# Routing in two mixture layers: normalisation per token, top two from raw logits, and another order of the steps around it

## The reference, cut to what matters

```python
x = x + 0.5 * _L0_ffn_ref(_layernorm(x, axis=-1), ...)    # F
x = x + _L0_attn_ref(_layernorm(x, axis=-1), ...)         # S
x = x + 0.5 * _L0_ffn_ref(_layernorm(x, axis=-1), ...)    # F
x = x + 0.5 * _L1_ffn_ref(_layernorm(x, axis=-1), ...)    # M
x = x + _L1_attn_ref(_layernorm(x, axis=-1), ...)         # U
x = x + 0.5 * _L1_ffn_ref(_layernorm(x, axis=-1), ...)    # M

def _L1_ffn_ref(x, w_router, w1, b1, w2, b2):             # 8 experts, top 2
    logits = xf @ w_router
    probs = jax.nn.softmax(logits, axis=-1)
    topk_w, topk_idx = jax.lax.top_k(probs, TOP_K)
    ...
    out = jnp.sum(out * weights[..., None], axis=1)
```

## Time and profile before

| | us |
|---|---|
| median of three runs | 1194.48 |
| lowest and highest run | 1188.43, 1200.24 |
| the profiled execution | 1189.11 |
| its span | 1187.3 |

### The profile page before, as it was taken

The page is one execution under the profiler, slowest core; times in us unless marked ns, Lnnn a source line. Parts: engine busy times, 40 slices in busy tenths (PEclk is TensorE's granted clock), DMA queues, the critical chain, the costliest instruction groups (busy, mean ns, idle before and its releaser), DMA issues.

```text
span 1187.3 us, 25908 instructions
## 1 busy us (share of the span) xinstructions
PE 1012.3 (85%) x9070; PEld 632.4 (53%) x9070; DVE 720.2 (61%) x1625; ACT 688.2 (58%) x1301; POOL 524.8 (44%) x405
## 2 busy tenths in 40 slices
PE   4788999999998876799999999999639968746995
PEld 1345555555555364355555555555339964325995
DVE  0577678777776653677776776876564423654441
ACT  2566686686673662676677667656316636623661
POOL 2664456556441542545444344433345530263451
PEclk9899999999999967999999999999759989857997
DMA  9895344455433600545444344432312240011223
GB/s 349 250 298 157 86 102 109 97 120 116 100 93 81 71 1 2 126 109 121 96 107 96 89 107 109 101 80 77 143 44 68 67 114 1 19 43 48 64 65 120
DMA packets 88511, 120.02 MB, mean 101 GB/s; under 512 B 20064, under 2 KB 72032, under 8 KB 87488
## 3 DMA queue, kind: packets, MB, share of 16 engines
q1 hardware_dynamic: 81824, 96.30, 33.8%
q0 software_dynamic: 6272, 20.44, 4.7%
q10 hardware_dynamic: 288, 1.63, 0.3%
HBM read 62.66 MB, written 22.11 MB: 71 GB/s over the span
## 4 chain that ended last, share of the span: by engine, by line
PE 65%; ACT 14%; issue 7%; DMA 6%; DVE 5%; POOL 1%; SPq 1%; ACTq 0%; DVEq 0%; POOLq 0%
PE banks L591 7%; PE banks L944 6%; PE banks L954 6%; PE banks L676 5%; PE banks L662 5%; PE banks L620 3%; PE banks L751 3%; PE banks L669 3%; PE banks L637 3%; PE banks L721 3%; PE banks L726 2%; PE banks L645 2%; DMA rstd<-arena 2%; ACT arena L1194 2%; ACT arena L1189 2%
## 5 line engine op out<-in xcount | busy, mean ns | idle before, releaser
L2041 POOL TENSOR_TENSOR arena<-arena 128x1024 f32<-128x1024 f32 x64 | 150.9, 2357 | 321.0 <-DVE arena L1644 318.7
L2030 POOL TENSOR_TENSOR arena<-arena 128x1024 f32<-128x1024 f32 x64 | 150.8, 2357 | 41.6 <-ACT arena L1189 41.6
L1636 DVE TENSOR_REDUCE arena<-banks 128x4 f32<-128x512 f32 x128 | 82.5, 686 | 93.5 <-PE banks L620 93.3
L1181 ACT ACTIVATE arena<-banks,arena 128x512 f32<-128x512 f32 x128 | 80.5, 679 | 93.6 <-PE banks L669 93.2
L591 PE MATMUL banks<-arena 128*128 128x512 f32 x256 | 128.6, 627 | 6.7 <-DVE arena L1563 5.9
L2020 POOL DMA_INDIRECT moe_outs<-arena x78 | 81.5, 1045 | 100.7 <-DVE arena L1882 88.6
L1386 ACT ACTIVATE arena<-banks,arena 128x128 f32<-128x128 f32 x312 | 89.0, 369 | 59.0 <-PE banks L944 58.9
L2013 POOL DMA_INDIRECT moe_rows<-arena x64 | 63.1, 986 | 118.5 <-DVE arena L1617 101.1
L1644 DVE TENSOR_TENSOR arena<-arena 128x1024 f32<-128x1024 f32 x64 | 78.1, 1220 | 28.4 <-DMA arena<-arena 28.4
L1194 ACT ACTIVATE arena<-banks 128x1024 f32<-128x1024 f32 x64 | 65.6, 1025 | 46.1 <-PE banks L591 45.1
L954 PE MATMUL banks<-arena 128*128 x624 | 87.5, 283 | 4.6 <-ACT arena L1386 4.4
(11 more groups left out here) (221 smaller groups left out, 1951.6 us busy)
## 6 DMA issues: line engine op xcount, KB each, us to landing
arena<-arena SPq DMA_DIRECT2D x256, 128.0 KB, 3.8
arena<-rstd SPq DMA_DIRECT2D x128, 256.0 KB, 4.3
moe_rows<-arena POOLq DMA_DIRECT2D x12, 903.0 KB, 6.6
arena<-moe_rows SPq DMA_DIRECT2D x78, 64.5 KB
arena<-in_rot SPq DMA_DIRECT2D x4, 1024.0 KB, 11.6
arena<-in_mw SPq DMA_DIRECT2D x2, 2048.0 KB, 10.8
arena<-moe_outs SPq DMA_DIRECT2D x16, 256.0 KB, 4.9
arena<-ssm_a SPq DMA_DIRECT2D x4, 512.0 KB, 6.6
```

The costliest lines, as they stand in the source:

```text
L1636: nc.vector.tensor_reduce(mx[:, e], by_row(bank[3 + e][:]), AX.X, ALU.max).then_inc(s_max, 1)
L2030: nc.gpsimd.tensor_tensor(TA[:, n % 2], RAW, ROTV[:, :, 0, c * C:(c + 1) * C], ALU.mult).then_inc(cos_done, 1)
L2041: nc.gpsimd.tensor_tensor(TA[:, n % 2], TA[:, n % 2], TB, ALU.add).then_inc(rot_sum, 1)
```

## The change

- The router weights are centred once: WRC = centre x WR, a matmul on PE (`centred_router`, L565 of the changed kernel) and a copy by DVE (L1546). The router's matmuls take X as it is and WRC (L571).
- The four transposes become four matmuls of X's tiles with `centre` (`token_rows`, L577), so tokens stand on partitions, centred but not yet scaled. DVE takes mean and variance of each token by `bn_stats` and `bn_aggr` (`moments`, L1572, L1576). ACT makes the inverse root of 128x4 values for a chunk and scales in the copy to XTOK: four copies of 128x128 for the first choice; the second choice is one copy of 128x512 from the first.
- The top two are taken from the unscaled logits (`pick`, L1553 to L1565: 5 chained steps in place of 10). The softmax of all tokens comes once for a mixture, `gates_start` behind the tile map, an exponential on ACT, and `gates_end` ahead of the diagonals.
- POOL scatters a chunk's four first choices when the first copy and the ranks are there, then the four second ones.
- The steps stand in another order on PE, DVE and ACT, in the tail of the second F as well as in U. Banks: `MX_TOK` and `MX_RANK` take the place of `MX_CEN` and `MX_VAR`.

```diff
@@ PE
+            def centred_router():
+                pe.wait_ge(moe_s_in, 48)
+                mm(bank[1][:, 0:NE], centre, WR, start=True, stop=True).then_inc(wrc, 1)
+
+            def route(moe, c):
+                pe.wait_ge(wrc, 2)
                 for t in range(TILES):
                     at = c * C + t * P
-                    last = mm(bank[MX_VAR[moe][c]][:, t * NE:(t + 1) * NE], YB[:, at:at + P], WR, start=True, stop=True)
+                    last = mm(bank[MX_RANK[moe][c]][:, t * NE:(t + 1) * NE], X[:, at:at + P], WRC, start=True, stop=True)
                 last.then_inc(router_mm, 1)
+
+            def token_rows(moe, c):
                 for t in range(TILES):
                     at = c * C + t * P
-                    last = nc.tensor.transpose(bank[MX_CEN[moe][c]][:, t * P:(t + 1) * P], YB[:, at:at + P], ident)
+                    last = mm(bank[MX_TOK[moe][c]][:, t * P:(t + 1) * P], X[:, at:at + P], centre, start=True, stop=True)
                 last.then_inc(xtok_mm, 1)
...
                     elif run:
                         pe.wait_ge(copied, 2 * n)
+                        pe.wait_ge(sq_done, n)
+                        centred_router()
                         pe.wait_ge(x_ffn, NCH + 1)
-                        centred(X, 0, MX_CEN[0][0])
+                        token_rows(0, 0)
...
                 if run:
-                    variance(mix, 0, MX_VAR[0][0])
+                    route(0, 0)
                 transpose_out(29, n - 3, s)
                 masks(31, n - 1)
                 values(30, n - 2, 0)
                 scores(31, n - 1)
                 values(30, n - 2, 1)
                 if run:
-                    pe.wait_ge(moe_s_in, 48)
-                    route(mix, 0, 0)
+                    rank(0, 0)
                 transpose_scores(31, n - 1)
...
                 unit_centred(3)
-                mix_centred(0)
-                mix_variance(0)
                 down(1)
+                enter(0)
                 unit_variance(3)
-                route(mix, 1, 0)
                 up(2, range(3))
-                mix_centred(1)
                 rank(1, 0)
-                mix_variance(1)
+                enter(1)
                 up(2, range(3, 4))
                 up(3)
-                route(mix, 1, 1)
+                rank(1, 1)
                 down(2)
                 down(3)
-                rank(1, 1)
-                mix_centred(2)
-                mix_variance(2)
-                route(mix, 1, 2)
-                mix_centred(3)
+                enter(2)
+                enter(3)
                 rank(1, 2)
-                mix_variance(3)
-                route(mix, 1, 3)
                 rank(1, 3)
@@ ACT
             def tokens(moe, c):
...
+                act.wait_ge(tok_dve, 2 * k + 2)
+                A(RSTD[:, tt], MOMENT[:, tt, 1], ACT.Ln, bias=eps_c).then_inc(tok_act, 1)
+                act.wait_ge(tok_act, 2 * k + 1)
+                A(RSTD[:, tt], RSTD[:, tt], ACT.Exp, scale=-0.5, bias=zero_c).then_inc(tok_act, 1)
...
+                for t in range(TILES):
+                    at = c * TILES + t
+                    last = A(XTOK[:, 0, at, 0:DM], bank[MX_TOK[moe][c]][:, t * P:(t + 1) * P], ACT.Copy, scale=RSTD[:, at:at + 1])
+                last.then_inc(xtok_done, 1)
+                act.wait_ge(xtok_done, 2 * k + 1)
+                A(XTOK[:, 1, tt, 0:DM], XTOK[:, 0, tt, 0:DM], ACT.Copy).then_inc(xtok_done, 1)
@@ DVE
                 normalise(31, n - 1)
                 if run:
-                    norm_chunks(mix, first_plain, [0])
+                    dve.wait_ge(cos_done, n)
+                    centred_router()
+                    moments(0, 0)
                 maximum(n - 1)
                 subtract(n - 1)
+                if run:
+                    pick(0, 0)
                 divide(n - 2)
-                if run:
-                    dve.wait_ge(cos_done, n)
-                    route(0, 0)
                 divide(n - 1)
...
                 if moe == 0:
-                    rank(0, 1)
-                    norm_chunks(norm0, first_plain, [2])
-                    route(0, 2)
                     rank(0, 2)
-                    norm_chunks(norm0, first_plain, [3])
-                    route(0, 3)
+                    pick(0, 3)
+                    moments(0, 3)
                     rank(0, 3)
                 tile_map()
+                gates_start(moe)
@@ POOL
-                    pool.wait_ge(xtok_done, 2 * k + 2)
                     pool.wait_ge(rank_dve, RANK_STEPS * (k + 1))
-                    for t in range(c * TILES, (c + 1) * TILES):
-                        for j in range(2):
+                    for j in range(2):
+                        pool.wait_ge(xtok_done, 2 * k + 1 + j)
+                        for t in range(c * TILES, (c + 1) * TILES):
```

More of the change, by code:

```diff
@@ L817, in ffn @@
                     pe.wait_ge(x_ffn, NCH + 2)
-                    centred(X, 1, MX_CEN[0][1])
+                    token_rows(0, 1)
+                    route(0, 1)
                 else:
@@ L830, in ffn @@
                 last_variance()
-                if run:
-                    variance(mix, 1, MX_VAR[0][1])
-                else:
+                if not run:
                     ssm_variance(0, 0)
@@ L837, in ffn @@
                 last_hidden(1)
-                if run:
-                    route(mix, 0, 1)
-                else:
+                if not run:
                     ssm_variance(1, 0)
                 last_hidden(2)
-                if not run:
+                if run:
+                    pe.wait_ge(xtok_done, 3)
+                    pe.wait_ge(rank_dve, 2 * RANK_STEPS)
+                    pe.wait_ge(x_ffn, NCH + 3)
+                    token_rows(0, 2)
+                    route(0, 2)
+                else:
                     ssm_centred(0, 1)
@@ L1289, in ffn @@
                 evacuate_out(31, n - 1, 0)
-                if run:
-                    norm_square(mix, 1, MX_CEN[0][1])
-                else:
+                if not run:
                     ssm_square(0, 0)
@@ L1310, in ffn @@
                 if run:
-                    tokens(0, 1)
+                    tokens(0, 2)
                 else:
@@ L1598, in route @@
[L1598 to L1600 removed]
+                for t in range(TILES):
+                    last = nc.vector.max(TOPL[:, c * TILES + t], part(moe, c, 0)[:, t])
+                chained(last, pick_dve)
+                for t in range(TILES):
+                    at = c * TILES + t
+                    last = nc.vector.max_index(TOPI[:, at], TOPL[:, at], part(moe, c, 0)[:, t])
@@ new lines, in pick, with moments @@
+                chained(last, pick_dve)
+                chained(nc.vector.tensor_copy(IDXF[:, tt], TOPI[:, tt]), pick_dve)
+                each = expert_id.unsqueeze(1).unsqueeze(1).to_broadcast([P, TILES, 2, NE])
+                chained(TT(OH[:, tt], each, IDXF[:, tt, 0:2].unsqueeze(3).to_broadcast([P, TILES, 2, NE]), ALU.is_equal), pick_dve)
+                chained(TT(MINE[:, tt], OH[:, tt, 0], OH[:, tt, 1], ALU.add), pick_dve)
+                assert n[0] == PICK_STEPS * (k + 1)
+            def moments(moe, c):
+                k = NCH * moe + c
+                dve.wait_ge(xtok_mm, k + 1)
+                for t in range(TILES):
+                    last = nc.vector.bn_stats(PART[:, c * TILES + t], bank[MX_TOK[moe][c]][:, t * P:(t + 1) * P])
+                last.then_inc(tok_dve, 1)
+                dve.wait_ge(tok_dve, 2 * k + 1)
+                for t in range(TILES):
+                    last = nc.vector.bn_aggr(MOMENT[:, c * TILES + t], PART[:, c * TILES + t])
+                last.then_inc(tok_dve, 1)
@@ L1763, in ffn @@
                 residual(7, gg - 1)
+                if run:
+                    pick(0, 1)
                 gate(6, gg - 2, 1)
+                if run:
+                    moments(0, 1)
                 gate(6, gg - 2, 2)
                 mlp_norm(7, gg - 1)
+                if run:
+                    rank(0, 1)
                 mlp_residual(6, gg - 2)
-                if run:
-                    norm_chunks(mix, first_plain, [1])
-                else:
+                if not run:
                     ssm_normed(0, 0)
@@ L1775, in ffn @@
                 if run:
-                    route(0, 1)
+                    pick(0, 2)
+                    moments(0, 2)
                 else:
```

174 lines of the change are left out of this document (66 added, 108 removed).

## The result

| | us |
|---|---|
| changed kernel, median of 4 runs (lowest, highest) | 1216.13 (1209.78, 1217.78) |
| kernel before, 4 runs beside them | 1191.86 (1188.43, 1200.24) |
| ratio, 95% interval | 1.0183 [1.0114, 1.0252] |
| the profiled execution after, its span | 1217.78, 1215.9 |

The changed kernel is slower by some 22 us (0.0183 x 1191.9; 14 to 30 by the interval), where the sum said 10.3. The two have most of their loss in common; that part is what the prediction is about. Whether the ratio itself differs is not shown, as the two intervals overlap; the traces of the two do differ.

The account below looks back on a forecast made before the run. PE's gapless chain in the second F's tail, then POOL's scatters, were taken as bounds. Terms: 22.6 - 10.7 - 1.6 = +10.3, giving 1199.4 from the profiled execution, 1204.8 by the median; 1202 put down, range 1189 to 1214.

Parts of the forecast that it names:

- C: Tail of second F: picks and ranks ahead of the last transposed scores, half clock included; +4.5, between 2.5 and 4.9.
- D: Rest of the tail: DVE's added picks, moments and ranks before the last residual, mostly fitting its waits; +2.1, 0 to 4.
- A: Head of step 32: PE waits for the router weights' load, then runs at half clock; +11.4, at least 9.0.
- B: Tail: copy of centred weights, router and three groups ahead of the last scores, half clock included; +4.6, 2.6 to 5.0.
- E: First routing's end: 16 back-to-back scatters, last starting 21.1 after the last residual in place of 31.8; -10.7.
- F: U and second routing: the scatter gap between chunks 2 and 3 goes, little else; -1.6, between -4 and +1.
- rival 2: Tail: clock doesn't recover between the three holes; +18.8, 1208 against the profiled execution, 1213 against the median; chance 0.18.
- Rival 3: Tail: PE's clock never falls at the waits; 6.4 less, so +3.9, 1193 and 1198; chance 0.15.
- Rival 4: Step 32: weights' wait is hidden by slack or they land at once; without A, -1.1; chance 0.12.
- slower by more than 12: Whole kernel: loss beyond the some 12 us that can be told from no change; chance 0.35.
- low end: Whole kernel: the terms' low ends sum to -0.6, giving 1188 from the lowest time; the range given starts at 1189.
- high end: Whole kernel: the terms' high ends, with -9.7 for the scatters, sum to +16.6, giving 1211 with the median.

Follow-up runs that it names:

- third group: Four old kernels run again unaltered on one chip: changed kernel 1202.40 (1.0126), kernel before 1185.62, and two partly moved-back versions, 1180.08 and 1189.42.
- third variant: Changed kernel with weights' wait, chunk 0's router, and chunk 0's picks and ranks moved back: 1192.79, 1.0016; timed again 1180.08, 0.9953.
- second group: Kernel before with three unused semaphores (1.0000); third variant with old semaphore order (0.9887), 8 unused columns (0.9950), or old scatter order (0.9936).
- first group: Four kernels undoing the changed kernel's moves one after the other, each keeping the earlier undoings: 1.0084, 1.0018, 1.0016, 1.0019 to the kernel before.
- first experiment: Changed kernel with the wait for the router weights moved from the head of step 32 to behind the loop: 1200.31, 1.0084.
- second variant: Changed kernel with the weights' wait behind the loop and chunk 0's router matmuls behind the last scores: 1193.02, 1.0018; timed again 1189.42, 1.0013.
- first variant: The kernel of the first experiment: changed kernel with only the weights' wait moved behind the loop, 1200.31, 1.0084.

## Why the prediction was right or wrong, point by point

Right: slower, for the reason given, three new waits of PE against back-to-back scatters. The size was short: 10.3 by the sum, 22 and 15 measured. Every term of the tail was too small, C and D most, and one cost was not in the profile of before at all. "First" is the trace of the result against the first of the kernel before, "again" the same pair in the third group (the three waits by their marks in the chains, the rest by the stretches).

| term | predicted | first | again |
|---|---|---|---|
| A, weights' wait | +11.4 | +12.2 | +12.0 |
| B, router ahead of the scores | +4.6 | +5.3 | +5.2 |
| C, ranks ahead of the transposed scores | +4.5 | +5.8 | +5.8 |
| D, rest of the tail | +2.1 | +5.3 | +3.3 |
| E, scatters behind the residual | -10.7 | -10.2 | -10.4 |
| F, U and second routing (U and R) | -1.6 | +9.8 | -0.9 |
| sum | +10.3 | +28.2 | +15.0 |

The sums leave out X (+3.5 and -3.1) and the moment at which the tail is reached (3.0 earlier, 1.7 later). With these the spans differ by 28.6 and 13.7.

- **A** was worked out as the wait and 2.4 for the clock, and came out nearly so (810.20 less 798.12, against 800.96 less 801.13: 12.2). The clock's part was 2.8 and not 2.4. The last load landed in 4.54 and 4.30. The Trainium skill ("DMA: Bandwidth & Descriptors", section "Anatomy of one DMA — SWDGE (gpsimd) path") has 2.0 as the fixed part alone and adds bytes / 436e9; for these 512 KB that would be 3.2, an estimate by that page, and 1.0 less than the trace's 4.2, not 2.2 as the prediction has it. The section is also about DMAs issued by GpSimd, and this one is SP's. Either figure is too short here.
- **B and C** ran at half clock nearly from end to end. Their clock cost 2.8 and 2.4 where 2.0 was put down; in C two records of L731 behind the transposed scores still took 1.71, not 0.86. C has a misreading as well: the transposed scores of before could go on behind the first half of the difference, not at 811.60, its end. Their row on PE's time line before:

```profile
811.06 1.25 PE L669 MATMUL banks<-arena 128*128 128x128 f32 x8
```

The picks now stand behind both halves, so 0.5 more is lost.
- **D** was too small (2.1; 3.3 again, and 5.3 first, where 1.89 is a late semaphore). The moments had the price forecast (0.89 + 0.38, predicted 1.4), but "most of the new work fits where DVE waited for PE" does not hold for the picks: in the third variant of the third group chunk 1's stand in the chain between output and gate (821.87 to 823.67). Without the three waits and without late semaphores T is still 2.3 (second group, three traces) to 3.7 (third group) above the kernel before. Moving chunk 1's work back won 1.2 in the first group, where semaphores were late in both traces; what the rest of D consists of is not isolated.
- **E** held to 0.5, with 21.6 predicted as 21.1. The chunks' second copies never held POOL up.
- **F** is the step that failed in the first trace. Without late semaphores it is -0.9 in the one pair: the last sum came 2.0 earlier, the last scatter 1.1 later behind it. That is partly luck. The last scatter was forecast 33 behind the sum and came 34.6 behind it in all six traces of the new routing without late semaphores (33.4 to 33.5 before), so this part costs 1.2 and wins nothing; and U is 156.3 to 163.9 in these six, so its -2.0 says little. With late semaphores the 8.6 of one update turned the sign. No row of before shows such a wait.
- **The rivals.** The clock doesn't stay low from B on (it is 1.00 at 824), so rival 2 falls, although the time came near its 1208 and 1213; the same number would have been taken for it without the stretches. Rival 3 falls with the stretches at 0.50: PE's pieces behind the three waits take 6.3, 6.4 and 6.0 (803.88 to 810.20, 817.25 to 823.61, 827.94 to 833.95), where the same ones at full clock take 3.6 and 3.5 by the prediction's rows and 3.6 in the third variant, so 8.0 together. The Trainium skill ("TensorE: Matmul & The Clock Gate", section "What's actually happening") advises leaving such ramps out, as under 1% of a span. The trace agrees with the share (0.7%), and yet it is over half of the 15 that the change costs. Rival 4 falls with the first experiment.
- **The number.** 1187.1 + 15.0 = 1202.1 is what these terms would give in the third group, and it measured 1202.4; that they meet so well is luck, as X and the arrival at the tail are left out. The recorded median, 1216.13, lies above the range's 1214, and the loss of 22 is the case "slower by more than 12", which had 0.35. By the prediction's own sum the low end is 1188 and not 1189, and the -9.7 of its high end has no working.
- **The difference between the two timings**, 14 us in the time and 7 us in the ratio, goes with late semaphores in the traces: 2.0 in D and 10.7 in F. The two waits without a releaser in the first trace (1.89 and 8.78) make 10.7 of these 12.7, and U's 2.0 are a part that I can't assign. Three kernels were timed both with late semaphores and without. The third variant's ratio fell clearly (1.0016 to 0.9953), the changed kernel's by as much but with overlapping intervals, and the second variant's not at all (1.0018 and 1.0013). So that the late semaphores make up the difference in time is argued and not shown, and what makes them late is open.

## What to carry to other kernels

Ask of every step that is moved forward what it waits for, and pay in full for the links behind it on an engine that has no gap there; add the clock that falls meanwhile (2.4 to 2.8 us here), once for each hole. A part of a change can be worth more than the change: the scatters' gain of 10 was real, and three small moves back kept it and made a kernel faster than both. When a ratio doesn't follow a stretch that clearly got shorter, run an unaltered kernel again on another chip before explaining the difference by an edit.

## What the runs showed of the hardware that I had not expected

- **Late semaphores.** In the five traces with holes an update of PE's arrives 1.5 to 8.6 us behind the row of its matmul. The waits for them begin while POOL issues indirect DMAs, but the longest ends 1.3 after the last of their landings on record (1063.78 against 1062.48 in the changed kernel). In the eight traces of the second and third group and in the first one of before no update of PE's is late by over 0.3. The holes are in the records of DVE's, ACT's and the DMA queues' updates as well. It goes by the group of runs and not by the kernel: the changed kernel and two variants were traced with and without. Some of the late updates fall on a scatter's recorded landing (1040.07 in the third variant), others lie between two (1048.68 in the first variant, between 1047.33 and 1048.97), so no rule comes of that.
- The recorder itself may be the brake. The Trainium skill ("NOTIFIC — the notification-queue block", section "7.1 Overflow: three behaviours, one of which stalls the engine") says that the block which writes the trace's records can drop them or hold back the engine that makes them when a queue is full. By that page it is one or the other, by a setting that software makes for all queues alike, so holes and late updates side by side do not simply follow from it. No run here tells a recorder that brakes from a slow semaphore path, and there is no time of an execution without a recorder.
- An expert stage that no edit touched differs by several us from trace to trace: X was 110.4 to 115.2 in the third group, and U, with the other mixture's experts, 156.3 to 163.9 in the three kernels there that share it. Differences of single spans of that size say nothing about an edit elsewhere; the stretch that holds the edit does, and medians of several runs help, though those of the second variant moved by more than its T.
